# A recurrence kernel: the mixes and the feeds of a tile put together, the projection cut in four

## The chip, the cores and the metric

One core of a Trainium2 chip runs the whole program. The metric is the device time of one execution in microseconds. Before the change it is 2249.52 us, the median of 3 runs (2249.39 to 2250.3).

## The reference

The input is x, 16 sequences of 512 tokens and 256 channels. Two layers run over it, each with a mixer and a feed-forward part behind a residual and a layer norm. Only the third part, the recurrence of layer 1, is touched by the change:

```python
        ms = jnp.mean(jnp.square(tokens), axis=-1, keepdims=True)
        x = tokens * jax.lax.rsqrt(ms + EPS) * norm_w
        x = x.reshape(B, T, H, D)
        a_t = jnp.tanh(a)
        def step(state, x_t):
            state = jnp.tanh(jnp.einsum('bhs,hst->bht', state, a_t) + jnp.einsum('bhd,hds->bhs', x_t, b))
            mixed = jnp.einsum('bhs,hsd->bhd', state, c) + skip[None] * x_t
            return (state, mixed)
        xs = jnp.moveaxis(x, 1, 0)
        _, outs = jax.lax.scan(step, state0, xs)
        return tokens + outs @ w_out.T + b_out
```

There are 16 heads with 16 channels and 64 states each, and 512 steps that must follow each other. The latent attention, the FP4 feed-forward and the channel mix around it are not changed.

## The kernel before, in words

Four stages follow each other: attention, the FP4 feed-forward, the recurrence, the channel mix. Each has its own program for every engine; semaphores are written by hand, and the order of an engine's instructions is the order in which the code emits them. The recurrence runs from about 1530 to 2047 us of the span.

It works on 64 tiles of 128 rows. A tile is 8 time steps (STEPS) of the 16 sequences. The state of all heads fills 4 PSUM banks, split in 2 sides of 2 banks. Step t of a tile goes: `recur` on TensorE multiplies the last state with A for side 0, then for side 1 (L1734, L1737; 8 calls a side, each on a 64x64 tile of the array, each shown as 2 matmul records and 2 weight loads), and ScalarE takes the tanh of each side (L1616) into the state. The next `recur` of a side waits for that tanh. The sums of B times the input were put in the same PSUM banks beforehand.

Around this cycle TensorE has side work for each tile, which sits in slots. A slot has the number at = 2t + q, behind the `recur` of step t and side q; all slots used in the loop are odd, so each stands behind side 1 of a step:

- `mix` (L1786, L1783), 2 calls for the 2 halves c of the channels: state times C for the tile before, on 128x32 tiles of the array. VectorE adds skip times x (outs, L1678).
- `project` (L1765): outs times w_out, 64x64 tiles. VectorE then adds z in two steps (L1692, L1694), takes its statistics (L1696, L1698), GpSimd makes 1/sqrt, and VectorE writes x3 (L1670) at the head of the next tile's work.
- `turn` (L1806): the normalised input of the next tile transposed; VectorE copies it scaled into xT (L1651).
- `inputs`, called the feed here (L1755, L1752): B times xT into the other set of sums for the next tile, on 32x64 tiles of the array, again for 2 halves c.

VectorE's order in a tile is: statistics of a later tile (L1636, L1638), x3, outs twice, xT, the normalisation (L1660), z and its statistics. TensorE's loop body holds 2 tiles. A `Fori` runs it once, then `fill` issues 32 matmuls on a quiet tile (L1774), and a second entry of the same code runs it 30 times more; tiles 0, 63 and 64 stand outside the loop. ScalarE's and VectorE's loops hold 4 tiles. Inside the loop a wait of TensorE counts from a register (`await_count`), outside it from a constant.

The slot table before is one line:

```python
        MIXES, PROJECTS, TURNS, FEEDS = (1, 3), (5, 9), 7, (13, 15)
```

So step 0 has mix 0, step 1 mix 1, step 2 projection 0, step 3 the turn, step 4 projection 1, step 5 nothing, step 6 feed 0, step 7 feed 1.

## Time and profile before

| | |
|---|---|
| median of 3 runs | 2249.52 us |
| the profiled execution, its own time | 2245.83 us |
| its span | 2244.1 us |
| TensorE matmul busy | 2186.6 us, 97% |
| VectorE busy | 1718.1 us, 77% |
| GpSimd busy | 1192.8 us, 53% |
| ScalarE busy | 1060.2 us, 47% |
| granted TensorE clock over the span | 0.993 |
| tanh of the recurrence (L1616) | 1024 instructions, 223 ns each |
| recurrence matmuls on L1734 | 8192 records, 219 ns each |

Busy means the union of an engine's records. On TensorE they overlap heavily: four 64x64 tiles of the array work side by side, a record lasts 219 ns and the next one starts some 14 ns later. So busy time and the duration of a record say little about how long a group of matmuls takes; the distance between starts says it. Times in rows are microseconds from the span's start, and durations of a few hundredths can be read from differences of starts in one view only.

### The profile page before, as it was taken

Reading aid. Unit: us, or ns where it says so; the run is one execution under the profiler, and the core shown is the slowest. Engines: PE = TensorE matmul, PEld = TensorE weight load, DVE = VectorE, ACT = ScalarE, POOL = GpSimd, SP = SyncE. Lnnn points to the kernel's source line nnn. Section 1 sums busy time; section 2 is a strip of 40 time slices with the busy share of each in tenths; the row PEclk is TensorE's granted clock in tenths of the full one; section 3 lists DMA queues with packets and bytes.
Section 4 is the critical chain, followed back from the end, with each engine's and each line's share of the span. In section 5 each row is a group of like instructions: output and inputs, shape, how many; then the busy total and the mean of one; then the engine's idle time right before and its main releaser. Section 6 shows DMA issues by size and latency. Waiting matters only on the chain.

```text
span 2244.1 us, 92167 instructions
## 1 busy us (share of the span) xinstructions
PE 2186.6 (97%) x37362; PEld 1540.2 (69%) x37362; DVE 1718.1 (77%) x4980; ACT 1060.2 (47%) x2707; POOL 1192.8 (53%) x1680
## 2 busy tenths in 40 slices
PE   9999999999999999999999999998999999999997
PEld 5566565656556555556777777777888888887775
DVE  5788888888887777769999999994555555556997
ACT  4655665656666665552222222222444444443444
POOL 4555555655655555536666666674344444442334
PEclk9999999999999999999999999998999999999999
DMA  4111111211121111111210101100011111111232
GB/s 150 58 49 58 67 63 63 67 58 58 67 67 58 68 58 58 50 52 31 68 33 30 33 31 32 42 24 29 28 33 36 34 33 33 37 49 38 87 94 76
DMA packets 101634, 117.83 MB, mean 53 GB/s; under 512 B 10672, under 2 KB 80080, under 8 KB 101456
## 3 DMA queue, kind: packets, MB, share of 16 engines
q1 hardware_dynamic: 101456, 115.44, 15.8%
q8 instruction: 113, 1.85, 0.4%
q14 instruction: 65, 0.53, 0.1%
HBM read 48.29 MB, written 33.55 MB: 36 GB/s over the span
## 4 chain that ended last, share of the span: by engine, by line
PE 92%; DVE 4%; issue 2%; ACT 1%; POOL 0%; DVEq 0%; ACTq 0%; POOLq 0%
PE ps_state L1734 10%; PE ps_down L1373 7%; PE ps_gate L1366 7%; PE ps_up L1366 7%; PE ps_near L812 6%; PE ps_far L592 5%; PE ps_near L584 5%; PE ps_far L584 4%; PE ps_near L592 3%; PE ps_far L627 3%; PE ps_far L611 3%; PE ps_far L604 3%; PE ps_state L1765 3%; PE ps_state L1737 2%; PE ps_r L2152 2%; PE ps_v L2163 2%
## 5 line engine op out<-in xcount | busy, mean ns | idle before, releaser
L1616 ACT ACTIVATE r_state<-ps_state 128x64 f32<-128x64 f32 x1024 | 228.4, 223 | 288.7 <-PE ps_state L1737 283.9
L1734 PE MATMUL ps_state<-r_state,later_pairs_a 64*64 64x32 f32 x8192 | 338.3, 219 | 24.4 <-ACT r_state L1616 11.7
L1734 PEld LDWEIGHTS ps_state<-r_state,later_pairs_a 64*64 64x64 f32 x8192 | 298.2, 135 | 76.1 <-issue 56.3
L1737 PE MATMUL ps_state<-r_state,later_pairs_a 64*64 64x32 f32 x8192 | 334.8, 220 | 1.2 <-issue 1.1
L480 DVE CUSTOM_DVE_ANT_0 ps_near<-ps_near,mask 128x512 f32<-128x512 f32 (+1 forms) x512 | 270.4, 589 | 83.6 <-PE ps_near L584 83.5
L340 POOL TENSOR_SCALAR_AFFINE_SELECT probsT<-probsT 128x512 f32<-128x512 f32 x256 | 160.6, 640 | 266.1 <-ACT probsT L460 168.2
L1737 PEld LDWEIGHTS ps_state<-r_state,later_pairs_a 64*64 64x64 f32 x8192 | 289.7, 135 | 0.4 <-issue 0.4
L480 DVE CUSTOM_DVE_ANT_0 ps_far<-ps_far,mask 128x384 f32<-128x384 f32 (+1 forms) x512 | 198.3, 457 | 33.6 <-PE ps_far L584 32.5
L1256 POOL TENSOR_TENSOR f_fp<-f_rounded,f_scale 128x960 f32<-128x960 f32 (+2 forms) x67 | 117.3, 1751 | 162.7 <-DVE f_rounded L1345 162.7
L1278 ACT ACTIVATE f_silu<-ps_gate 128x704 f32<-128x704 f32 x64 | 48.4, 757 | 285.8 <-PE ps_gate L1366 285.8
L592 PE MATMUL ps_far<-Q,K 32*128 32x256 f32 (+2 forms) x1536 | 181.2, 416 | 1.2 <-ACT probsT L457 0.5
L1373 PE MATMUL ps_down<-kept_w_downT,f_hT 128*128 128x256 f32 x768 | 176.7, 380 | 1.5 <-ACT f_hT L1283 1.5
L460 ACT ACTIVATE probsT<-ps_far 128x512 f32<-128x512 f32 x256 | 132.2, 603 | 90.0 <-PE ps_far L598 90.0
L584 PE MATMUL ps_near<-K,Q 32*128 32x512 f32 (+1 forms) x1024 | 162.7, 518 | 1.7 <-DVE bias_row L498 0.8
L592 PEld LDWEIGHTS ps_far<-Q,K 32*128 32x128 f32 x1536 | 129.6, 184 | 49.6 <-issue 24.7
L1366 PE MATMUL ps_gate<-kept_w_upT,f_xT 128*128 128x352 f32 x512 | 162.1, 460 | 1.4 <-DVE z L487 0.9
L1366 PE MATMUL ps_up<-kept_w_upT,f_xT 128*128 128x352 f32 x512 | 162.1, 460 | 0.0
L1581 POOL TENSOR_TENSOR r_veps<-r_mv,r_eps 128x1 f32<-128x1 f32 x64 | 12.2, 190 | 280.2 <-DVE r_mv L1698 280.2
L1373 PEld LDWEIGHTS ps_down<-kept_w_downT,f_hT 128*128 128x128 f32 x768 | 141.1, 190 | 18.5 <-ACT f_hT L1283 1.9
L812 PE MATMUL ps_near<-probsT,V 128*32 128x512 f32 (+3 forms) x2048 | 151.1, 436 | 0.8 <-ACT probsT L427 0.8
L329 POOL TENSOR_TENSOR k_sin<-K,cos_sin 128x512 f32<-128x512 f32 x64 | 81.1, 1268 | 131.2 <-ACT K L418 131.2
L480 DVE DVE_READ_ACCUMULATOR2_ANT top<- 128x1 f32 x1024 | 142.6, 139 | 0.0
(218 smaller groups left out, 5411.7 us busy)
## 6 DMA issues: line engine op xcount, KB each, us to landing
q_swap<-q_sin SPq DMA_DIRECT2D x128, 128.0 KB, 2.1
k_swap<-k_sin SPq DMA_DIRECT2D x128, 128.0 KB, 2.1
xT<-in_xT_dram SPq DMA_DIRECT2D x16, 512.0 KB, 3.7
xtok<-in_x_dram SPq DMA_DIRECT2D x16, 512.0 KB, 3.8
x_rows<-x SPq DMA_DIRECT2D x16, 512.0 KB, 2.9
f_x<-x_rows SPq DMA_DIRECT2D x64, 128.0 KB, 2.1
x_rows<-f_x SPq DMA_DIRECT2D x64, 128.0 KB, 1.8
r_x<-x_rows SPq DMA_DIRECT2D x64, 128.0 KB, 2.1
```

The costliest lines, as they stand in the source:

```text
L340: return nc.gpsimd.affine_select(block, block, pattern=[[0, GROUP], [1, P]], compare_op=ALU.is_ge, fill=0.0, base=0, channel_multiplier=-1)
L460: nc.scalar.activation(mine[:, t, AT[1]:AT[1] + SEQ], far[t], ACT.Exp).then_inc(exped, 1)
L480: nc.vector.tensor_tensor_reduce(bank[:, at:at + width], bank[:, at:at + width], mask[:, SEQ - width:SEQ], 1.0, -3e38, ALU.add, ALU.max, t ...
L584: out = nc.tensor.matmul(bank[:, at:at + width], Q[rows, g, qi * P:(qi + 1) * P], K[rows, g, 0:width], start=True, stop=True, skip_group_c ...
L592: return nc.tensor.matmul(bank[:, at:at + SEQ - kj * P], K[rows, g, kj * P:(kj + 1) * P], Q[rows, g, kj * P:SEQ], start=(kj != 3), stop=Fa ...
L812: out = nc.tensor.matmul(near[0][LATENT * t:LATENT * (t + 1), kj * P:SEQ], V[:, jp, kj, head_of(gp, t), :], probsT[:, gp % 2, t, AT[kj]:AT ...
L1256: nc.gpsimd.tensor_tensor(blocks(parts(fp4[:, s, :], i, BLOCK)), blocks(parts(rounded[:, s, :], i, BLOCK)), spread(parts(scale[:, s, :], i ...
L1366: out = nc.tensor.matmul(ps[:, half, 0:HALF], xT[:, j % 2, c, :], w_upT[:, c, at + half * HALF:at + (half + 1) * HALF], start=(c == 0), st ...
L1373: out = nc.tensor.matmul(ps_down[:, 0:DIM], hT[:, j % 2, kd, :], w_downT[:, kd, :], start=(kd == 0), stop=(kd == KD - 1))
L1616: nc.scalar.activation(state[:, j % 2, banks, :, t, 0, :], sums[j % 2][:, banks, :, now], ACT.Tanh).then_inc(state_ready[t], 1)
L1734: nc.tensor.matmul(sums[j % 2][half(v), stays, c, now], A[half(v), 3 * q, c, :], last[half(v), stays, c, :], start=False, stop=True, skip_ ...
L1737: out = nc.tensor.matmul(sums[j % 2][half(1 - v), changes, c, now], A[half(v), 3 * q + 1 + was, c, :], last[half(v), changes, c, :], start ...
```

## The change

The two mixes of a tile stand behind each other in slot 1 (step 0). The projection is cut by output columns (n) and by channel half (c) in four pieces of 4 calls with 128 columns, where there were two of 4 calls with 256; the pieces go to slots 3, 7, 9 and 11 (steps 1, 3, 4, 5). The turn goes to slot 5 (step 2), in tile 0 it stays in slot 7. Both feeds stand behind each other in slot 15 (step 7). Steps count from 0 here; step 6 has no side work now. The last tile has its pieces in slots 3, 4, 5 and 6. A piece waits for outs only where n is 0. VectorE's, ScalarE's, GpSimd's and the DMA queues' programs stay as they are. The inner matmuls of the mix stand at L1789 and L1786 in the changed file, the projection at L1768, the turn at L1812.

```diff
--- before.py
+++ after.py
@@ -1756,15 +1756,18 @@
                                              start=(c == 0), stop=False, skip_group_check=True)
             return out
 
-        def project(j, c, states):
-
-            s = (j - 1) % 2
-            await_count(outs_ready, states[c])
+        def project(j, piece, states):
+
+
+            s, n, c = (j - 1) % 2, piece // CC, piece % CC
+            columns = slice(n * P, (n + 1) * P)
+            if n == 0:
+                await_count(outs_ready, states[c])
             for tokens in range(2):
                 for r in range(2):
-                    out = nc.tensor.matmul(room[s][half(tokens), OUT[r], :], outs[half(r), s, c, half(tokens)], w_outT[half(r), c, :],
+                    out = nc.tensor.matmul(room[s][half(tokens), OUT[r], columns], outs[half(r), s, c, half(tokens)], w_outT[half(r), c, columns],
                                            start=(c == 0), stop=(c == CC - 1), skip_group_check=True)
-            if c == CC - 1:
+            if piece == 2 * CC - 1:
                 out.then_inc(out_full, 1)
 
         def fill(j, bank, times, start):
@@ -1786,9 +1789,12 @@
                         nc.tensor.matmul(into, C[:, 3 * (bank // 2), c, :], state[:, s, bank, c, :, 0, :], start=True, stop=True)
             return out
 
-        MIXES, PROJECTS, TURNS, FEEDS = (1, 3), (5, 9), 7, (13, 15)
-
-        LAST_PROJECTS, MIXING = (5, 7), 11
+
+        MIXES, PROJECTS, TURNS, FEEDS = 1, (3, 7, 9, 11), 5, 15
+
+        FIRST_TURNS = 7
+
+        LAST_PROJECTS, MIXING = (3, 4, 5, 6), 11
 
         def first_turn():
 
@@ -1818,32 +1824,29 @@
                     if exists(i, 0):
                         recur(j, t, q, states)
                     at = SIDES * t + q
-                    if at in MIXES and not first:
-                        if at == MIXES[0]:
-                            for side in range(SIDES):
-                                await_count(state_ready[STEPS - 1], states[side])
-                        mix(j, MIXES.index(at)).then_inc(mix_full, 1)
-                    if at == TURNS and exists(i, 1):
+                    if at == MIXES and not first:
+                        for side in range(SIDES):
+                            await_count(state_ready[STEPS - 1], states[side])
+                        for c in range(CC):
+                            mix(j, c).then_inc(mix_full, 1)
+                    if at == (FIRST_TURNS if first else TURNS) and exists(i, 1):
                         await_count(xn_ready, next_tile)
                         await_count(outs_ready, states[1])
                         if first:
                             pe.wait_ge(*fed[1])
                         turn(j)
-                    if at in projects and not first:
-                        project(j, projects.index(at), states)
+                    for piece in range(2 * CC):
+                        if at == projects[piece] and not first:
+                            project(j, piece, states)
                     if at == MIXING and last:
                         pe.wait_ge(z_added, TILES)
                         mixing.to(0)
-                    if at in FEEDS and exists(i, 1):
-                        c = FEEDS.index(at)
-                        if c == 0:
-                            await_count(xT_ready, next_tile)
-                            await_count(z_added, this_tile)
-                            if first:
-                                pe.wait_ge(*fed[1])
-                        out = inputs(j, c)
-                        if c == CC - 1:
-                            out.then_inc(inputs_in, 1)
+                    if at == FEEDS and exists(i, 1):
+                        await_count(xT_ready, next_tile)
+                        await_count(z_added, this_tile)
+                        for c in range(CC):
+                            out = inputs(j, c)
+                        out.then_inc(inputs_in, 1)
 
             for t in range(STEPS):
                 if first and t == LAST_FED:
```

TensorE's rows at the head of the loop, before, from the last matmuls of step 0's `recur` to those of step 1 (L1786 and L1783 are the mix, L1734 and L1737 the recurrence):

```order
L1737 MATMUL ps_state<-r_state,later_pairs_a 64x32 x2
L1786 MATMUL ps_state<-r_state,later_pairs_c 32x128
L1783 MATMUL ps_state<-r_state,later_pairs_c 32x4x16
L1786 MATMUL ps_state<-r_state,later_pairs_c 32x128
L1783 MATMUL ps_state<-r_state,later_pairs_c 32x4x16 x3
L1734 MATMUL ps_state<-r_state,later_pairs_a 64x32 x2
```

The same place in the changed kernel (L1789 and L1786 are now the mix):

```order
L1737 MATMUL ps_state<-r_state,later_pairs_a 64x32 x2
L1789 MATMUL ps_state<-r_state,later_pairs_c 32x128
L1786 MATMUL ps_state<-r_state,later_pairs_c 32x4x16
L1789 MATMUL ps_state<-r_state,later_pairs_c 32x128
L1786 MATMUL ps_state<-r_state,later_pairs_c 32x4x16 x3
L1789 MATMUL ps_state<-r_state,later_pairs_c 32x128
L1786 MATMUL ps_state<-r_state,later_pairs_c 32x4x16
L1789 MATMUL ps_state<-r_state,later_pairs_c 32x128
L1786 MATMUL ps_state<-r_state,later_pairs_c 32x4x16 x3
L1734 MATMUL ps_state<-r_state,later_pairs_a 64x32 x2
```

The second mix moved up past the 16 calls of step 1's `recur` and stands behind the first without a recurrence matmul between.

TensorE's rows around projection 0, before: it stood behind side 1 of step 2 (L1765):

```order
L1734 MATMUL ps_state<-r_state,later_pairs_a 64x32 x2
L1737 MATMUL ps_state<-r_state,later_pairs_a 64x32 x2
L1765 MATMUL ps_state<-later_w_outT,r_outs 64x256 x4
L1734 MATMUL ps_state<-r_state,later_pairs_a 64x32 x2
L1737 MATMUL ps_state<-r_state,later_pairs_a 64x32 x2
```

And in the changed kernel, behind side 1 of step 1:

```order
L1734 MATMUL ps_state<-r_state,later_pairs_a 64x32 x2
L1737 MATMUL ps_state<-r_state,later_pairs_a 64x32 x2
L1768 MATMUL ps_state<-later_w_outT,r_outs 64x128 x4
L1734 MATMUL ps_state<-r_state,later_pairs_a 64x32 x2
L1737 MATMUL ps_state<-r_state,later_pairs_a 64x32 x2
```

A piece has as many calls as a projection had, with half the columns; there are four a tile, so 8 calls more a tile than before.

## Rows read from the trace of the kernel before

**Rows 1.** The page: busy time by engine, and the chain by engine.
```profile
PE 2186.6 (97%) x37362; PEld 1540.2 (69%) x37362; DVE 1718.1 (77%) x4980; ACT 1060.2 (47%) x2707; POOL 1192.8 (53%) x1680
...
PE 92%; DVE 4%; issue 2%; ACT 1%; POOL 0%; DVEq 0%; ACTq 0%; POOLq 0%
```

**Rows 2.** A window of 30 us; busy (records) by engine, PEclk, DMA share, GB/s.
```profile
1571.00:1601.00 30.00, 29.01 (x1371) 25.13 (x1368) 15.14 (x52) 13.39 (x60) 10.04 (x24) 1.00 0.09 27
```

**Rows 3.** ScalarE's timeline: start, length, line, records, idle before; steps 0 to 7, 0.
```profile
1696.23 0.46 ACT L1616 ACTIVATE r_state<-ps_state 128x64 f32<-128x64 f32 x2 [0.93 <-PE ps_state L1737]
1697.15 0.46 ACT L1616 ACTIVATE r_state<-ps_state 128x64 f32<-128x64 f32 x2 [0.46 <-PE ps_state L1737]
1698.11 0.46 ACT L1616 ACTIVATE r_state<-ps_state 128x64 f32<-128x64 f32 x2 [0.50 <-PE ps_state L1737]
1699.01 0.46 ACT L1616 ACTIVATE r_state<-ps_state 128x64 f32<-128x64 f32 x2 [0.44 <-PE ps_state L1737]
1699.87 0.46 ACT L1616 ACTIVATE r_state<-ps_state 128x64 f32<-128x64 f32 x2 [0.40 <-PE ps_state L1737]
1700.77 0.46 ACT L1616 ACTIVATE r_state<-ps_state 128x64 f32<-128x64 f32 x2 [0.44 <-PE ps_state L1737]
1701.63 0.46 ACT L1616 ACTIVATE r_state<-ps_state 128x64 f32<-128x64 f32 x2 [0.40 <-PE ps_state L1737]
1702.69 0.46 ACT L1616 ACTIVATE r_state<-ps_state 128x64 f32<-128x64 f32 x2 [0.61 <-PE ps_state L1737]
1703.79 0.45 ACT L1616 ACTIVATE r_state<-ps_state 128x64 f32<-128x64 f32 x2 [0.64 <-PE ps_state L1737]
```

**Rows 4.** TensorE's timeline around mix 0 (step 0).
```profile
1703.68 0.23 PE L1737 MATMUL ps_state<-r_state,later_pairs_a 64*64 64x32 f32 x2
1703.84 0.30 PE L1786 MATMUL ps_state<-r_state,later_pairs_c 128*32 128x128 f32 x1
...
1703.97 0.27 PE L1786 MATMUL ps_state<-r_state,later_pairs_c 128*32 128x128 f32 x1
...
1704.20 0.25 PE L1734 MATMUL ps_state<-r_state,later_pairs_a 64*64 64x32 f32 x2
```

**Rows 5.** TensorE's timeline around feed 1 (step 7).
```profile
1702.79 0.32 PE L1755 MATMUL ps_state<-r_xT,later_pairs_b 32*64 32x128 f32 x1
...
1702.95 0.27 PE L1755 MATMUL ps_state<-r_xT,later_pairs_b 32*64 32x128 f32 x1
...
1703.20 0.24 PE L1734 MATMUL ps_state<-r_state,later_pairs_a 64*64 64x32 f32 x1
```

**Rows 6.** TensorE's timeline: the turn (step 3), a projection (step 2), recurrence behind each.
```profile
1699.13 0.46 PE L1806 MATMUL ps_state<-kept_ident,r_xn 64*64 64x64 f32 x16
1699.38 0.21 PE L1734 MATMUL ps_state<-r_state,later_pairs_a 64*64 64x32 f32 x1
...
1705.64 0.64 PE L1765 MATMUL ps_state<-later_w_outT,r_outs 64*64 64x256 f32 x8
1706.11 0.20 PE L1734 MATMUL ps_state<-r_state,later_pairs_a 64*64 64x32 f32 x2
```

**Rows 7.** VectorE's timeline: z, x3 and the first outs.
```profile
1700.68 0.41 DVE L1692 TENSOR_TENSOR r_z<-ps_state,r_x_twice 128x256 f32<-128x256 f32 x1
...
1703.31 0.41 DVE L1670 TENSOR_SCALAR r_x<-r_z,r_mv,r_rstd 128x256 f32<-128x256 f32 x1
1704.36 0.35 DVE L1678 SCALAR_TENSOR_TENSOR r_outs<-r_xT,later_recurrence_columns,ps_state 128x128 f32<-128x128 f32 x1 [0.64 <-PE ps_state L1783]
```

**Rows 8.** DMA: PE's code queue q8 in 1541 to 1571; the only one in 1571 to 2013.
```profile
q8 instruction: 6, 0.10, 1.3%
...
q14 instruction: 2, 0.02, 0.0%
```

**Rows 9.** TensorE's timeline: where two stalls of the first pass end.
```profile
1555.32 0.24 PE L1734 MATMUL ps_state<-r_state,later_pairs_a 64*64 64x32 f32 x2 [2.19 <-issue]
...
1565.04 0.19 PE L1737 MATMUL ps_state<-r_state,later_pairs_a 64*64 64x32 f32 x1 [1.06 <-issue]
```

## The prediction

> **What bounds the kernel now.** I read four views in this order. The page: TensorE is busy 97% of the span and 92% of the chain that ended last is PE [rows 1]. That is a busy share of overlapping records, so it does not say whether the recurrence waits for the array or for the loop through ScalarE. The windows: in the recurrence the granted clock is 1.00, its upper level of 2.4 GHz, and 1371 matmul records run in 30 us [rows 2]. The timeline of ScalarE gives the answer. Its tanh pair starts once a step, so the distance of two starts is the length of a step, and what TensorE does between them is known from the slot table. One tile reads 0.92, 0.96, 0.90, 0.86, 0.90, 0.86, 1.06, 1.10 us for steps 0 to 7, 7.56 in all [rows 3]. Step 5 has no side work at all, step 3 has the turn, and both take 0.86. So 0.86 is a floor set by the way PE, ScalarE, PE, and every step above it is set by TensorE's own work: steps 0 and 1 (one mix each), 2 and 4 (one projection each), 6 and 7 (one feed each). Under the floor there is free room on TensorE: the turn occupies it from 1699.13 to 1699.38, 0.25 us, and costs nothing [rows 6].
>
> **The question of the change** is then simple: a piece of side work is free if it fits in a step's room, and costs its full length when the room is already used. Moving work out of a step can win no more than that step's excess over 0.86.
>
> **Projections.** One projection is 8 records of 256 columns, from 1705.64 to the next recurrence matmul at 1706.11: 0.47 us, excess 0.04 (0.90 less 0.86) [rows 3, 6]. A piece has the same 8 records with 128 columns, so about 0.24 us, if it goes by columns as the row's length suggests. That is the turn's size, which is free. Steps 1, 3, 4 and 5 now carry one piece each and step 2 the turn. Bounds for a piece: 0 (the turn) and 0.04 (a whole projection), I take 0. Steps 2 and 4 give back 0.04 each: **-0.08**. The 8 extra calls a tile and their weight loads lie in the same room.
>
> **Mixes.** Before: 0.92 and 0.96. In step 1 the mix goes and a piece comes: 0.96 to 0.86, **-0.10**. Step 0 gets the second mix behind the first. Its price: a mix runs its 128 columns in two passes, first start 1703.84, second pass 1703.97, 0.13 each, so 0.26 for another; with the way out to the next recurrence matmul (1704.20) it is 0.36 [rows 4]. The projection's 0.47 for 256 columns in two passes gives 0.24 for 128. So the bounds are 0.24 and 0.36 and I take 0.26, as the passes are this operation's own: **+0.26**. Nothing hides it: step 0 is already above the floor.
>
> The way from a recurrence matmul into a mix shows 0.16 us between starts (1703.68 to 1703.84) [rows 4]. Merging leaves out one way in and one way out, and the two terms hold this already, because the marginal price has neither in it. What merging wins there is spent again on the floor: the freed step cannot get below 0.86.
>
> **Feeds.** Step 6 falls from 1.06 to the floor: **-0.20**. Step 7 gets the second feed. A feed starts at 1702.79, its second pass at 1702.95, the next recurrence matmul at 1703.20 [rows 5]. Two passes are 0.26 (at 0.13) to 0.32 (at 0.16); outer bounds 0.24 by the projection's columns and 0.41 if merging saved nothing. I take **+0.28**. The two waits ahead of the feeds move to step 7 with them; such a wait at the head of a group is worth 0 to 0.06 (steps 0 and 1 with the same work differ by 0.04), I take **+0.04**.
>
> **Sum of a tile:** -0.08 - 0.10 + 0.26 - 0.20 + 0.28 + 0.04 = **+0.20 us**, so 7.56 becomes 7.76. The cause is plain: before, two rooms swallowed part of a mix and two rooms part of a feed; now one room does in each case, and step 6 stands empty. 60 tiles of the loop run in steady state: 60 x 0.20 = +12.0 us.
>
> **Ends of the loop.** The first two tiles of the loop are held up by code loading: their stalls end at 1555.32 and 1565.04, and by my count of the built program 512 instructions lie between, 9.72 us or 19 ns each [rows 9]; side work is free there. The change adds 8 calls to each of the two tiles in the body, and a call is 2 matmuls and 2 weight loads, so 64 instructions: 1.2 us once, and I put 0.6 us for the last two tiles, whose code is fresh too. Tiles 0 and 64 have no excess that moves. Together **+13.8 us**. The profiled execution took 2245.8 us (span 2244.1); it would become 2259.6. The median of the runs shown lies 3.7 us above it: 2249.5 + 13.8 = **2263.3 us**. A measurement of this kernel can tell about 0.2% (4.5 us) from no change.
>
> **Who waits for whom.** The last piece now ends in step 5, one step later. z starts 0.81 us after the tanh of step 4 (1700.68 against 1699.87), x3 2.63 after z, and x3 runs 0.41 [rows 3, 7]. Moved by a step, x3 ends about 3.7 to 3.85 us after the tanh of step 5; the tanh of the next step 0 comes 0.86 + 0.86 + 1.42 = 3.1 after it, the first outs 0.57 later at 3.7 (1704.36 against 1703.79). So x3 and the first outs, in VectorE's order, just touch. Outs takes 0.35 and is wanted by the first piece 1.2 us after the tanh of step 0: ready at 0.92 to 1.1. Price 0, with little cover; if the cover is gone, the rival below. z itself is ready some 0.3 us before the feeds of step 7 ask for it. The queue behind PE's new wait for outs in step 1 holds the whole recurrence.
>
> **Rivals.**
> 1. **Code of the loop has to be loaded again** (24%). In steady state no packet of PE's code queue is seen, only 2 of 8 KB for others in 442 us, while 6 packets with 0.10 MB, so 16 KB and 256 instructions each, came in the first pass [rows 8]. The stalls mark where blocks begin: the one that ends at 1555.32 stands before instruction 802 of the loop by my count, so blocks begin at 34, 290 and so on to 1570. By that count the old loop and the 32 warming matmuls behind it end within 7 blocks, 5 instructions short of an eighth. The new loop (1561 instructions, it was 1497) still ends 9 short, but the warming block crosses, and the block ahead of it is then fetched too. If that pushes out the loop's first block, the jump back loads again: one block, a stall of 1 to 2.2 us [rows 9], which is 2265; or all of it, (9.72 - 5.6) x 3 = 12 us, which is 2275 (5.6 us is what 512 instructions take in steady state, at 2739 records in 30 us [rows 2]). The Trainium skill, page Runtime: NRT & Kernel Launch, section Instruction fetch mechanics, gives PE 2048 instructions in blocks of 256, and a stall for a taken branch out of them; the trace agrees that a loop of 1497 stays in.
> 2. **The loop itself crosses the edge** (3%). My 9 instructions are wrong and every jump reloads: 30 x 12 us, about 2620.
> 3. **The second group is nearly free** (5%, the faster side). The 0.13 us between the passes of a mix would then be a wait for the array to empty, as the 0.16 us of the way in are, and a second group of the same shape would run inside it: 0.26 less 0.16 is 0.10 for each group, a tile at 0.20 - 0.16 - 0.18 = -0.14, 60 x -0.14 + 1.8 = -6.6, 2242.9. It decides below 0.17 for each group. For it: the ways in and out (0.16 us in, 0.23 from the second pass to the next recurrence matmul) are wider than the 0.13 within. Against it: the projection, which changes no shape, also takes 0.24 for 128 columns in two passes [rows 6]. The Trainium skill, page TensorEngine Tiling (Array Packing), section Key Properties, says that changing the tiling mode drains the engine. By that rule the two merged groups save two drains on the way in and two on the way out, and it speaks for the change; the trace agrees that there is a gap of 0.16 us between 64x64 and 128x32 tiles.
> 4. **VectorE comes late** (8%). The first piece waits for outs, 0.1 to 0.2 us a tile: 2269 to 2275. For it: the touch above. Against: a step with a piece needs TensorE for 0.90 - 0.24 = 0.66 of its 0.86, so step 1 has 0.2 us of room even then.
> 5. **Nearly nothing changes** (5%): groups at 0.20 or less each: +0.06 a tile or less, 2255 or under; nearly all of it within 0.2%. The spacing of starts inside a group, some 10 ns, speaks for it, the passes against it.
>
> **How the numbers follow.** Forecast 55%, 2263.3. With groups at 0.24 a tile costs 0.14 and the time is 2249.5 + 8.4 + 1.8 = 2259.7; the low end goes on into rival 5, as far as groups at 0.20 with +0.06 a tile, 3.6 + 1.8 = 5.4: 2255. The high end takes in rivals 1 and 4 (2275) and groups at 0.36 (+0.38 a tile, 22.8 + 1.8: 2274): 2276. Left out are rivals 2 and 3 and some tails. Faster by over 0.2%: 0.05; within 0.2%: 0.04; slower by over 0.2%: 0.91.
>
> **What would show it.** ScalarE's starts in a new tile: 1.18, then six steps of 0.86, then 1.42, 7.76 in all. Two mixes 0.26 apart and two feeds 0.28 apart. PE's code queue silent again after the warming block. Wrong: step 1 above 0.9 with PE waiting for outs; step 0 at 1.0 (rival 3); 16 KB packets inside the loop (rivals 1, 2); freed steps below 0.8.

## The result, and the profile after

The changed kernel takes 2293.99 us, the median of 4 runs (2291.68 to 2296.67), against 2249.45 us for the kernel before beside it (4 runs, 2247.72 to 2250.3): ratio 1.0204, interval 1.0191 to 1.0218. It is 44.5 us slower. The prediction said slower, but 13.8 us, and its range ended at 2276.

The profiled execution took 2295.57 us (span 2293.8, granted clock 0.984 where it was 0.993). Its page, TensorE's code queue first in the list of queues:

```profile
PE 2223.2 (97%) x38386; PEld 1566.7 (68%) x38386; DVE 1716.6 (75%) x4980; ACT 1064.1 (46%) x2707; POOL 1192.2 (52%) x1680
...
q8 instruction: 122, 2.00, 0.4%
...
PE 92%; DVE 4%; issue 2%; ACT 1%; POOL 0%; DMA 0%; DVEq 0%; ACTq 0%; SPq 0%; POOLq 0%
```

Beside [rows 1] the busy shares and the chain say nothing: PE is 97% and 92% in both. The two things to see are the 1024 matmul records more (8 calls x 2 records x 64 tiles) and 122 packets on q8, TensorE's code queue. The page of before has 113 there:

```profile
q8 instruction: 113, 1.85, 0.4%
```

 Two views find the 44.5 us, one for the loop in steady state and one for its first tiles.

**Steady state.** ScalarE's timeline of a whole pair of tiles (starts of step 7, then 0 to 7, then 0 to 7 of the next tile):

```profile
1684.43 0.46 ACT L1616 ACTIVATE r_state<-ps_state 128x64 f32<-128x64 f32 x2 [0.39 <-PE ps_state L1737]
1686.07 0.43 ACT L1616 ACTIVATE r_state<-ps_state 128x64 f32<-128x64 f32 x2 [1.18 <-PE ps_state L1737]
1687.17 0.46 ACT L1616 ACTIVATE r_state<-ps_state 128x64 f32<-128x64 f32 x2 [0.67 <-PE ps_state L1737]
1688.03 0.46 ACT L1616 ACTIVATE r_state<-ps_state 128x64 f32<-128x64 f32 x2 [0.40 <-PE ps_state L1737]
1688.92 0.46 ACT L1616 ACTIVATE r_state<-ps_state 128x64 f32<-128x64 f32 x2 [0.44 <-PE ps_state L1737]
1689.79 0.46 ACT L1616 ACTIVATE r_state<-ps_state 128x64 f32<-128x64 f32 x2 [0.40 <-PE ps_state L1737]
1690.65 0.46 ACT L1616 ACTIVATE r_state<-ps_state 128x64 f32<-128x64 f32 x2 [0.40 <-PE ps_state L1737]
1691.51 0.46 ACT L1616 ACTIVATE r_state<-ps_state 128x64 f32<-128x64 f32 x2 [0.40 <-PE ps_state L1737]
1692.36 0.46 ACT L1616 ACTIVATE r_state<-ps_state 128x64 f32<-128x64 f32 x2 [0.39 <-PE ps_state L1737]
1694.19 0.23 ACT L1616 ACTIVATE r_state<-ps_state 128x64 f32<-128x64 f32 x1 [1.38 <-PE ps_state L1737]
...
1695.53 0.46 ACT L1616 ACTIVATE r_state<-ps_state 128x64 f32<-128x64 f32 x2 [0.68 <-PE ps_state L1737]
```

The tile from 1686.07 reads 1.10, 0.86, 0.89, 0.87, 0.86, 0.86, 0.85, 1.83 us for steps 0 to 7: 8.12. The next one has 1.34 in step 0 and 1.64 in step 7, 8.16. (The one ends with the loop's jump back in step 7, and part of the jump's cost shows in step 0 of the next.) Over the later tiles of the loop the mean tile is 8.14 us; the same mean before is 7.73, since its tiles are not all as short as the 7.56 of [rows 3]: 0.41 a tile.

**The first tiles.** From the first tanh of a tile to that of the next, tiles 0 to 5 took 11.05, 11.91, 19.50, 7.55, 7.76 and 7.74 us before, 65.5 together; after 11.10, 18.15, 20.28, 17.95, 12.98 and 9.44, 89.9 together. That is 24.4 us more in six tiles, of which 6 x 0.41 = 2.5 belong to the steady price. So about **22 us** are a thing of the loop's start, and about **25 us** (62 x 0.41) the steady price. Of the 22, 16 lie in tiles 3 to 5 (40.4 us where they took 23.1, less 3 x 0.41) and 6 in tiles 1 and 2 (38.4 where they took 31.4, less 2 x 0.41). Windows, after and then before (busy and records by engine; granted clock, DMA share, GB/s):

```profile
1541.00:1571.00 30.00, 22.98 (x785) 20.83 (x768) 8.57 (x29) 8.13 (x34) 6.96 (x18) 0.66 0.10 29
1571.00:1612.00 41.00, 28.66 (x835) 25.28 (x830) 9.12 (x30) 7.56 (x34) 8.53 (x22) 0.71 0.06 17
1612.00:1642.00 30.00, 29.13 (x1360) 25.32 (x1350) 14.37 (x49) 12.88 (x58) 11.18 (x26) 0.94 0.11 34
```

```profile
1541.00:1571.00 30.00, 24.36 (x728) 20.35 (x729) 8.45 (x29) 7.30 (x33) 9.26 (x23) 0.77 0.13 38
1571.00:1612.00 41.00, 39.59 (x1888) 34.35 (x1885) 21.26 (x71) 18.40 (x83) 15.25 (x39) 1.00 0.09 26
```

In the same 41 us from 1571 there are 835 matmul records where there were 1888, and the granted clock is 0.71 instead of 1.00. The DMA queues of after name the reason, in 1541 to 1571, in 1571 to 1612, and all that is left of code loading in 1612 to 2080:

```profile
q8 instruction: 5, 0.08, 1.2%
```

```profile
q8 instruction: 10, 0.16, 1.8%
```

```profile
q14 instruction: 2, 0.02, 0.0%
```

TensorE's code comes in 16 KB blocks on q8. Before, the first pass of the loop brought in the loop's blocks and the one behind them [rows 8], and no packet came after it until the loop's end. Now that block, in which the warming matmuls end, comes at 1571.3, and one more behind it at 1575.2; counted from the one in which the loop begins it is the ninth. Right behind it come eight packets from 1576.7 to 1610.1: the loop's whole code a second time. TensorE's timeline shows the place:

```profile
1571.06 0.61 PE L1777 MATMUL ps_state<-r_quiet 128*128 128x256 bf16 x4
1574.05 4.88 PE L1777 MATMUL ps_state<-r_quiet 128*128 128x256 bf16 x28 [2.39 <-issue]
1580.00 0.25 PE L1734 MATMUL ps_state<-r_state,later_pairs_a 64*64 64x32 f32 x2 [1.06 <-issue]
...
1583.03 0.32 PE L1734 MATMUL ps_state<-r_state,later_pairs_a 64*64 64x32 f32 x2 [2.60 <-issue]
```

The group of warming matmuls (L1777) stops after 4 of its 32 matmuls. By the prediction's count the loop ends 9 instructions short of an edge, and four matmuls with their weight loads are eight. The two rows behind it with a wait for issue are the loop's own head, whose code had been loaded 40 us earlier. So **rival 1 happened**, in its whole form.

### The profile page after: what moved, and what is told of

Same layout as the page of the kernel before. It is cut to its first block, busy times and chain, and to the rows that moved or that the text cites. A ratio compares the mean times of both kernels' runs of the same rounds, so it can differ in the third digit from the quotient of the medians.

```text
span 2293.8 us, 94215 instructions
## 1 busy us (share of the span) xinstructions
PE 2223.2 (97%) x38386; PEld 1566.7 (68%) x38386; DVE 1716.6 (75%) x4980; ACT 1064.1 (46%) x2707; POOL 1192.2 (52%) x1680
## 4 chain that ended last, share of the span: by engine, by line
PE 92%; DVE 4%; issue 2%; ACT 1%; POOL 0%; DMA 0%; DVEq 0%; ACTq 0%; SPq 0%; POOLq 0%
PE ps_state L1734 10%; PE ps_down L1373 7%; PE ps_gate L1366 6%; PE ps_up L1366 6%; PE ps_near L812 6%; PE ps_far L592 5%; PE ps_near L584 5%; PE ps_far L584 4%; PE ps_state L1737 3%; PE ps_state L1768 3%; PE ps_near L592 3%; PE ps_far L627 3%; PE ps_far L611 3%; PE ps_far L604 3%; PE ps_k L2134 2%; PE ps_r L2155 2%
## 5 line engine op out<-in xcount | busy, mean ns | idle before, releaser
L1734 PE MATMUL ps_state<-r_state,later_pairs_a 64*64 64x32 f32 x8192 | 351.3, 221 | 27.4 <-issue 14.2
L1734 PEld LDWEIGHTS ps_state<-r_state,later_pairs_a 64*64 64x64 f32 x8192 | 307.4, 137 | 87.2 <-issue 75.0
L1737 PE MATMUL ps_state<-r_state,later_pairs_a 64*64 64x32 f32 x8192 | 347.4, 222 | 0.0
L1737 PEld LDWEIGHTS ps_state<-r_state,later_pairs_a 64*64 64x64 f32 x8192 | 293.1, 137 | 0.0
L460 ACT ACTIVATE probsT<-ps_far 128x512 f32<-128x512 f32 x256 | 132.5, 605 | 89.9 <-PE ps_far L598 89.9
```

The lines of the kernel that those rows point to most:

```text
L460: nc.scalar.activation(mine[:, t, AT[1]:AT[1] + SEQ], far[t], ACT.Exp).then_inc(exped, 1)
L1734: nc.tensor.matmul(sums[j % 2][half(v), stays, c, now], A[half(v), 3 * q, c, :], last[half(v), stays, c, :], start=False, stop=True, skip_ ...
L1737: out = nc.tensor.matmul(sums[j % 2][half(1 - v), changes, c, now], A[half(v), 3 * q + 1 + was, c, :], last[half(v), changes, c, :], start ...
```

## The experiments

A step's length below is the distance of ScalarE's starts in steady state, a pair's length the distance from the first row of a group of side work to the next recurrence row on TensorE. "Ahead of the loop" always means this edit, which moves all code behind it by n/2 instructions (two waits become one):

```diff
+        for _ in range(n):
+            pe.wait_ge(set_up, 1)
         with pe.Fori(0, 2) as again:
```

| kernel | median us (runs) | ratio to before, interval |
|---|---|---|
| the change | 2293.99 (4) | 1.0204, 1.0191 to 1.0218 |
| a_pad40 | 2301.95 (4) | 1.0294, 1.0214 to 1.0374 |
| a_pad100 | 2276.86 (4) | 1.0132, 1.0117 to 1.0147 |
| a_fill0 | 2266.16 (4) | 1.0079, 1.0064 to 1.0095 |
| a_feed8 | 2249.84 (8) | 1.0010, 1.0000 to 1.0020 |
| a_feed16 | 2275.59 (2) | 1.0123, 1.0105 to 1.0142 |
| a_feed10 | 2272.64 (1) | |
| a_feed12c | 2273.65 (1) | |
| b_feeds | 2262.96 (4) | 1.0070, 1.0050 to 1.0089 |
| b_mixes | 2253.93 (7) | 1.0036, 1.0023 to 1.0050 |
| b_pad12 | 2250.54 (10) | 1.0021, 1.0011 to 1.0031 |
| b_pad60 | 2255.53 (12) | 1.0046, 1.0026 to 1.0067 |
| b_pad100 | 2249.72 (11) | 1.0010, 1.0002 to 1.0019 |
| b_spread | 2253.32 (11) | 1.0023, 1.0014 to 1.0032 |
| b_spread_fill0 | 2247.60 (11) | 1.0006, 0.9995 to 1.0017 |
| b_fill0 | 2243.04 (12) | 0.9981, 0.9971 to 0.9991 |

### Where the blocks of code lie

**a_pad40**: the change with n = 40 ahead of the loop.

> The changed kernel with 40 waits that are long satisfied ahead of TensorE's loop, so that by the count of instructions the loop and the warming matmuls behind it end within seven blocks of 256 (the loop begins at place 6 of a block, ends at 1567, the warming block at 1633 of 1792). Theory A (the jump back out of the warming block found the loop's first blocks thrown out, and all of it was loaded again): the code packets of TensorE in 1541 to 1620 fall from 17 to about 8, tiles 3 and 4 run at 8.1 to 8.2 us, and the time falls by 18 to 25 us, to 2269 to 2276. Rival B (the slow first tiles come from the change's own order in code that is fresh): the packets and the time stay within 4 us of 2294.

The edit is 20 instructions and not 40 as the expectation counts (94235 in the trace, 94215 in the change). So it is not the test that was meant: the crossing isn't taken away, the loop itself now ends 11 behind the edge. Measured: 2301.95 us (one of four runs at 2335.39, hence the wide interval), 8 us more than the change, and 122 packets on q8 as in the change: the reload is there, with eight packets from 1578.3 to 1613.5 behind a ninth block at 1575.3. The first six tiles take 99.7 us together, 9.8 more than in the change. Its queue list for 1625 to 2080, where the loop runs in steady state, has no q8 at all:

```profile
q1 hardware_dynamic: 16896, 15.47, 10.8%
q14 instruction: 1, 0.01, 0.0%
```

So a loop that runs over the edge into an eighth block (14 instructions, six whole blocks, 11 instructions) does not load again at every jump; its mean tile is 8.13 us, as in the change. Rival 2 of the prediction would have been false even where its premise holds. A loop over nine blocks wasn't run.

**b_pad12**: the kernel before with n = 12 ahead of the loop.

> The kernel before with 12 satisfied waits ahead of the loop: the warming block now crosses into an eighth block by 7 instructions, the loop itself does not. Theory A: 16 KB packets go on after the warming block, tiles 3 to 5 are slow, and the time rises by 15 to 25 us to 2265 to 2275. Rival B: twelve waits cost under 1 us, 2249 to 2251.

Six instructions, so the warming matmuls with the jump behind them cross the edge by one. 2250.54 us and 113 packets on q8: nothing loaded again. Its mean tile is 7.80 us instead of 7.73, which makes the 4 us; the difference lies in the steps with the jump back.

**a_pad100**: the change with n = 100, by which the loop starts on place 16 and nothing crosses.

> The changed kernel with 50 instructions of satisfied waits ahead of TensorE's loop (two waits made one instruction, so the earlier run with 40 waits moved the blocks by 20 only and pushed the loop itself over an edge). Now the loop begins at place 16 of a block and the warming matmuls end at 1643 of 1792. Theory A (whole reload once, after the warming block has crossed into an eighth block and a ninth was fetched): 17 code packets in 1541 to 1620 fall to 8, tiles 3 to 5 run at 8.0 to 8.2 us from the start, 19 to 25 us less than the changed kernel, 2269 to 2275. Rival B (the slow tiles 3 to 5 belong to the change's order): within 4 us of 2294.

2276.86 us, 17.1 less than the change, though 50 instructions were added; 113 packets on q8. Tiles 3 to 5 take 24.1 us together, 16 less than in the change, and the mean tile is 8.02 us where it was 8.14, which is 7 us more; tile 0 gives back 6, as it takes 16.9 us behind the added instructions. In the window in which the change had 835 matmul records and a clock of 0.71:

```profile
1571.00:1612.00 41.00, 38.20 (x1568) 32.46 (x1568) 16.69 (x56) 14.60 (x66) 13.40 (x32) 0.89 0.09 27
```

This shows that the reload hangs on where the code lies, not on the order of the work.

**b_pad60**: the kernel before with n = 60; the warming matmuls with their jump cross by 25.

> The kernel before with 30 instructions of satisfied waits ahead of the loop: the loop ends inside the seventh block, the warming block crosses by 25 instructions (with 6 instructions, by one, nothing was loaded again). Theory A: eight more 16 KB packets behind the warming block, tiles 3 to 5 slow, 15 to 25 us more, 2262 to 2272. Rival B: 2247 to 2252.

2255.53 us, with a mean tile of 7.82 us, and the profiled execution has 113 packets and no reload, against the expectation. One of the 12 runs took 2282.66 us, 27 above the median; it wasn't profiled, so whether it was a reload stays open. In the change they cross by 59 (5 short before, and 64 instructions more). In the traces the reload goes with a ninth block, counted from the one in which the loop begins, fetched before the loop is entered again (both executions with 122 packets), and crossing by few instructions fetches no ninth block. Where the border between 25 and 59 lies wasn't tried.

**b_pad100**: the kernel before with n = 100.

> The kernel before with 50 instructions of satisfied waits: loop at place 16, warming block ends at 1579 of 1792, nothing crosses. Theory A: no packet after the warming block, and the first pass as before. The edges of the blocks move within the loop, and the time of the jump back (0.42 us a pair of tiles before, 0.33 to 0.56 in the runs so far) may move by 0.15 either way: 2242 to 2254.

2249.72 us: nothing gained and nothing lost within the bound. Its steady tile is 7.67 us instead of 7.73, as a stall of 0.256 us at the head of every fourth tile is gone, but its first tile takes 16.7 us instead of 11.05. Between a_pad100 and b_pad100, both without crossing and with the loop at the same place, the steady difference is 8.02 - 7.67 = **0.35 us a tile**, and the whole difference 27.1 us: 20 in the 56 tiles behind the first six, 5 in the first six, the rest at the ends. That is the price of the change itself, clear of where its code lies.

**a_fill0**: the change without the 32 warming matmuls. The line stands in the outer loop, so it takes out two groups, the one between the two entries and a second one behind the loop.

```diff
-            fill(0, TURN[0], 32, False)
```

> The changed kernel without the 32 warming matmuls behind each pass of the outer loop. The loop then ends 7 instructions short of the edge and nothing enters the eighth block. Theory A: no whole reload, 17 us less as in a_pad100, and the two groups of warming matmuls, 5 and 4 us, fall away too: 2268 to 2275, if the clock recovers by itself within a few tiles. Rival B (reload has nothing to do with the warming block): 2285 to 2290.

2266.16 us, 27.8 below the change, 113 packets on q8. Tiles 0 to 3 take 11.1, 17.87, 12.02 and 8.26 us, and the tile behind the loop 8.00 where it took 11.44: the second group alone is 3.4 us. Nothing crosses now, so nothing loads again, and the clock in the second window is at its upper level without the warming matmuls:

```profile
1571.00:1612.00 41.00, 38.77 (x1868) 33.31 (x1868) 20.41 (x69) 17.89 (x80) 16.57 (x40) 1.00 0.10 33
```

The whole differences, 17.1 and 27.8 us, hold other things beside the reload. Tiles 3 to 5 price it alone: 40.4 us in the change, 24.1 in a_pad100, 24.5 in a_fill0, so **16 us** from either side. The other 6 of the loop's 22 lie ahead of it, and tile 1 makes them: it takes 18.15 us in the change and 17.87 in a_fill0, where before it took 11.91, so the first pass is slow with the reload and without. The granted clock was lower there than before (0.66 against 0.77 in 1541 to 1571), and a_pad100 has 14.8 with the same calls; why wasn't tried. Tile 2, which holds the stalls of 2.39 and 1.06 us shown above, is only 0.8 longer than before.

### What each part of the change costs

**b_mixes**: the kernel before with both mixes in slot 1. (Of the diffs here and below only the main lines are shown.)

```diff
-        MIXES, PROJECTS, TURNS, FEEDS = (1, 3), (5, 9), 7, (13, 15)
+        MIXES, PROJECTS, TURNS, FEEDS = 1, (5, 9), 7, (13, 15)
```

> The kernel before with the mixes alone put together in slot 1. Forecast by the columns' passes: step 0 +0.26, step 1 from 0.96 to 0.86, +0.16 a tile, +10 us, 2259. By what the changed kernel shows (step 0 +0.19, and +0.1 more where the loop jumps back): +0.1 to 0.15 a tile, +6 to 9 us, 2255 to 2259.

2253.93 us, +0.10 us a tile. Step 1 is 0.86, step 0 is 1.13 in the tile that begins without the jump. The pair of mixes in the change, to be read against [rows 4]:

```profile
1686.08 0.30 PE L1789 MATMUL ps_state<-r_state,later_pairs_c 128*32 128x128 f32 x1
...
1686.33 0.27 PE L1789 MATMUL ps_state<-r_state,later_pairs_c 128*32 128x128 f32 x1
...
1686.67 0.25 PE L1734 MATMUL ps_state<-r_state,later_pairs_a 64*64 64x32 f32 x2
```

From 1686.08 to 1686.67 are 0.59 us, where one mix took 0.36: the second costs 0.23. The second mix starts 0.25 behind the first. The predicted 0.26 stands almost as put.

**b_feeds**: the kernel before with both feeds in slot 15.

```diff
-        MIXES, PROJECTS, TURNS, FEEDS = (1, 3), (5, 9), 7, (13, 15)
+        MIXES, PROJECTS, TURNS, FEEDS = (1, 3), (5, 9), 7, 15
```

> The kernel before with the feeds alone put together in slot 15 (loop length 1497, no crossing). If the second feed costs what the changed kernel shows, step 6 falls by 0.16 to 0.21 and step 7 rises by 0.45 to 0.54, +0.3 us a tile, 60 tiles: +18 us, 2267 to 2268. If merged feeds cost only their columns (my forecast, +0.12 a tile): +7 us, 2257.

2262.96 us, +0.22 us a tile: by far the dearer part. Step 6 falls to 0.85, but step 7 takes 1.60 in one tile and 1.84 in the other. TensorE's timeline of the change around the pair, to be read against [rows 5]:

```profile
1684.39 0.21 PE L1737 MATMUL ps_state<-r_state,later_pairs_a 64*64 64x16 f32 x2
1684.64 0.29 PE L1755 MATMUL ps_state<-r_xT,later_pairs_b 32*64 32x128 f32 x1
...
1685.27 0.28 PE L1752 MATMUL ps_state<-r_xT,later_pairs_b 32*64 32x64 f32 x5
1685.48 0.25 PE L1734 MATMUL ps_state<-r_state,later_pairs_a 64*64 64x32 f32 x2
```

From 1684.64 to 1685.48 are 0.84 us; one feed took 0.41 [rows 5]. The second feed costs 0.43 us, as much as the first one with its way out, though it has no way out of its own. The way in, 0.25 us here, holds the two waits.

The two parts alone come to 0.32 us a tile, the whole change to 0.41, or to 0.35 with the blocks aligned alike. So the projection in four pieces and the moved turn, which were to give back 0.08, give back nothing that this sum shows. It can't show 0.04, though: where the code lies alone moves the mean tile by up to 0.15 (7.67 to 7.82 with n = 0 to 100).

### Why the second feed costs 0.43

A feed has 12 calls: banks 0 and 2 take one call of 128 columns for each v (2 each), banks 1 and 3 two calls of 64 strided columns, by parity (4 each). Four kernels change only that.

**a_feed8**: all four banks in whole calls; the exchange by parity of banks 1 and 3 is left out.

```diff
-                        if bank % 2:
-                            out = nc.tensor.matmul(steps_of(sums[s][half(v ^ parity), bank, c, :], parity), B[rows, 2 * c + v, :], steps_of(xT_now, parity),
-                                                   start=(c == 0 and parity == 0), stop=False, skip_group_check=True)
-                        elif parity == 0:
-                            nc.tensor.matmul(sums[s][half(v), bank, c, :], B[rows, 2 * c + v, :], xT_now,
-                                             start=(c == 0), stop=False, skip_group_check=True)
+                        if parity == 0:
+                            out = nc.tensor.matmul(sums[s][half(v), bank, c, :], B[rows, 2 * c + v, :], xT_now,
+                                                   start=(c == 0), stop=False, skip_group_check=True)
```

> The changed kernel with 8 calls of 128 columns in each feed in place of 12 (4 of 128, 8 of 64): the parity exchange of every second bank is left out, so these banks get their inputs in the wrong order; the columns that stream through each tile of the array are the same, 128 a feed. Theory C (the second feed is bound by how fast instructions come, 9 ns each): it costs 32 x 9 = 0.29 us in place of 0.43, and step 7 falls by 0.14 to 0.25 as the first feed shrinks too. Rival D (bound by columns or by draining): step 7 unchanged within 0.04. The loop is 64 instructions shorter and crosses nothing, so tiles 3 to 5 are not slow.

```profile
1697.23 0.70 PE L1752 MATMUL ps_state<-r_xT,later_pairs_b 32*64 32x128 f32 x32
1697.97 0.25 PE L1734 MATMUL ps_state<-r_state,later_pairs_a 64*64 64x32 f32 x2
```

These rows are of a tile with the jump back: 0.74 us from the first row of the pair to the recurrence, where the change takes 1.16; in the tile without it it is 0.63, where the change takes 0.84. The last start is 0.43 behind the first. Step 7 is 1.40 and 1.43, and the kernel takes 2249.84 us, 27 less than a_pad100, as much as the kernel before. 17 of the 27 are the steady tiles (7.72 us against 8.02); the rest lie in the loop's first tiles and at its end (this kernel has fewer instructions and no added waits). The tile with the jump wins most: 1.84 to 1.43. So split calls are a good part of what makes the merged feeds dear. What a second feed of whole calls costs behind a first is not measured, as no kernel here has one such feed alone.

**a_feed16**: all four banks in split calls (n = 40 ahead of the loop; with the calls added ahead of it the loop begins on place 50, so nothing crosses).

```diff
-                        if bank % 2:
-                            out = nc.tensor.matmul(steps_of(sums[s][half(v ^ parity), bank, c, :], parity), B[rows, 2 * c + v, :], steps_of(xT_now, parity),
-                                                   start=(c == 0 and parity == 0), stop=False, skip_group_check=True)
-                        elif parity == 0:
-                            nc.tensor.matmul(sums[s][half(v), bank, c, :], B[rows, 2 * c + v, :], xT_now,
-                                             start=(c == 0), stop=False, skip_group_check=True)
+                        to = v ^ parity if bank % 2 else v
+                        out = nc.tensor.matmul(steps_of(sums[s][half(to), bank, c, :], parity), B[rows, 2 * c + v, :], steps_of(xT_now, parity),
+                                               start=(c == 0 and parity == 0), stop=False, skip_group_check=True)
```

> The changed kernel with 16 calls of 64 columns in each feed in place of 12 calls, the same columns and the same result, and 20 instructions of waits ahead of the loop so that nothing crosses (17 code packets fall to 9). Against a_pad100 (step 7 of an odd tile 1.60 us): Theory C (the supply of instructions, 9 ns each): 2 x 16 instructions more, step 7 at 1.85 to 1.90, 15 to 20 us more than a_pad100, 2292 to 2297. Rival D (columns or draining): step 7 at 1.60 to 1.64, 2277 to 2280.

```profile
1701.10 0.92 PE L1752 MATMUL ps_state<-r_xT,later_pairs_b 32*64 32x64 f32 x64
1701.95 0.25 PE L1734 MATMUL ps_state<-r_state,later_pairs_a 64*64 64x32 f32 x2
```

0.85 us for 16 calls a feed where 12 took 0.84. A third more instructions cost nothing in this tile, so the supply of instructions is not the limit there. In the tile with the jump back the pair takes 1.21 us for 1.16, and the mean tile is 8.07 for 8.02.

**a_feed12c**: 12 calls, but banks 1 and 3 are split in the first and the second 64 columns instead of by parity, so they get other inputs (n = 100).

```diff
+                        part = half(parity)
...
-                            out = nc.tensor.matmul(steps_of(sums[s][half(v ^ parity), bank, c, :], parity), B[rows, 2 * c + v, :], steps_of(xT_now, parity),
+                            out = nc.tensor.matmul(sums[s][half(v ^ parity), bank, c, part], B[rows, 2 * c + v, :], xT_now[:, part],
```

> The changed kernel with the same 12 calls of a feed, but the split calls take 64 columns that lie side by side instead of every second group of 16 (the banks with an exchange get wrong inputs), and 50 instructions of waits so that nothing crosses. Theory E: the pair still spans 0.66 to 0.70. Theory F (the strided reading or writing of the split calls is what costs): 0.43 to 0.50, and the time falls by 10 us or more against a_pad100's 2276.9.

2273.65 us (a single run), and the pair's last start lies 0.70 us behind its first, exactly as in the change. The stride is not the reason.

**a_feed10**: bank 3 whole, bank 1 split: 10 calls a feed.

```diff
-                        if bank % 2:
+                        if bank == 1:
```

> The changed kernel with 10 calls in a feed: bank 1 keeps its two calls of 64 columns a half, bank 3 gets one call of 128 (its parity exchange is left out, so its inputs are in the wrong order). The pair of feeds spans 0.697 us from first to last start with 12 and with 16 calls and 0.43 with 8. Theory E (the strip of 32 rows with most weight loads sets it: 8 a feed in a strip with split calls, 4 in one without): 0.66 to 0.70, as one strip still has 8. Theory G (the number of calls above 8): 0.56 to 0.60.

The last start is 0.59 to 0.62 us behind the first, the kernel takes 2272.64 us (a single run). With 0, 1, 2 and 4 banks split the same distance is 0.43, 0.59, 0.70 and 0.70 us. The theory of the busiest strip (0.66 to 0.70) falls by this, and that of the number of calls (0.56 to 0.60) fits here but not at 16 calls. So the split lengthens the pair, and how it does so stays open.

### Spreading instead of merging

If merging costs, cutting the feed finer could win. **b_spread** puts the 24 feed calls of a tile in three groups of 8, in slots 11, 13 and 15 of the kernel before (steps 5, 6, 7).

```diff
-        MIXES, PROJECTS, TURNS, FEEDS = (1, 3), (5, 9), 7, (13, 15)
+        MIXES, PROJECTS, TURNS, FEEDS = (1, 3), (5, 9), 7, (11, 13, 15)
...
+        PARTS = ([p for p in EVERY if p[2] % 2 and p[0] == 0],
+                 [p for p in EVERY if not p[2] % 2 and p[0] == 0] + [p for p in EVERY if p[2] % 2 and p[0] == 1 and p[1] == 0],
+                 [p for p in EVERY if not p[2] % 2 and p[0] == 1] + [p for p in EVERY if p[2] % 2 and p[0] == 1 and p[1] == 1])
```

> The kernel before with the same 24 feed calls of a tile in three groups of 8, in slots 11, 13 and 15 (slot 11 takes banks 1 and 3, whose readers are done; z is waited for at slot 13), the opposite of putting them together. Theory (each step has free room, and a group pays only what goes over it): step 5 rises from 0.86 to 0.88 to 0.95, steps 6 and 7 fall by 0.09 to 0.14 each, -0.1 to -0.2 us a tile, 6 to 12 us less than before, 2237 to 2243. Rival (each group of another array shape pays its way in and out, 0.16 us and more, so a third group costs what it saves): within 4 us of before.

2253.32 us, 0.2% slower, against the expectation and as its rival had it. ScalarE's starts of steps 5, 6, 7 and the next 0:

```profile
1692.23 0.46 ACT L1616 ACTIVATE r_state<-ps_state 128x64 f32<-128x64 f32 x2 [0.44 <-PE ps_state L1737]
1693.23 0.46 ACT L1616 ACTIVATE r_state<-ps_state 128x64 f32<-128x64 f32 x2 [0.54 <-PE ps_state L1737]
1694.19 0.46 ACT L1616 ACTIVATE r_state<-ps_state 128x64 f32<-128x64 f32 x2 [0.51 <-PE ps_state L1737]
1695.25 0.42 ACT L1616 ACTIVATE r_state<-ps_state 128x64 f32<-128x64 f32 x2 [0.60 <-PE ps_state L1737]
```

They are 1.00, 0.96 and 1.06, together 3.02, where before they are 0.86, 1.06 and 1.10 [rows 3], also 3.02. A group of 8 calls starts 0.15 us behind the recurrence, runs 0.18 between its first and last start and needs 0.20 to the next recurrence row: 0.53, where 12 calls need 0.56. Two thirds of a small group are its ways in and out, so a third of the work less saves nearly nothing. (The group in slot 11, all of split calls, runs 0.24 and needs 0.15 behind it: 0.54.) Spreading ends where the ways outweigh the work. The mean tile is 7.79 us against 7.73, and the longest step is step 0 behind the jump (1.16 for 1.04), where the placing of the code acts too.

**b_spread_fill0**, the same without the warming matmuls:

> The feeds in three groups and no warming matmuls. If the clock recovers by itself: 5 to 8 us under b_spread. If the recurrence stays at the lower clock without them: steps of 1.28 us as in the slow tiles, far above 2300.

2247.60 us, 5.7 less than b_spread, at the same mean tile (7.79). The gain is that of the warming matmuls alone, which the last kernel takes up.

### A version that beats both

**b_fill0**: the kernel before without the line `fill(0, TURN[0], 32, False)`.

> The kernel before without the 32 warming matmuls behind each of the two passes of the outer loop; nothing else. With the feeds in three groups their removal gave 5.7 us (2253.3 to 2247.6), and steps came down from 1.28 to 0.86 within two tiles by themselves. The same here: 5 to 7 us less than before, about 2241.

2243.04 us, ratio 0.9981 (0.9971 to 0.9991), 5 us less than the kernel before beside it. Tiles 0 to 4 take 11.05, 13.33, 15.60, 10.79 and 7.81 us, and in steady state all is as before (7.73). The first six tiles come to 66.3 us where they were 65.5, and the tile behind the loop takes 7.62 where it took 11.10. The clock lies a little lower at first than in the kernel before (0.94 against 1.00) and is at 1.00 from 1612 on:

```profile
1571.00:1612.00 41.00, 39.49 (x1821) 34.11 (x1813) 21.01 (x70) 18.01 (x80) 15.82 (x39) 0.94 0.08 26
```

So in the two profiled executions the first group, 5.3 us long, about pays for itself. What is saved is the second group behind the loop, 3.5 us, which stands there since the line is in the outer loop, and which the clock did not need: it is at 1.00 before it and behind it, with the group and without. The profiled executions differ by 2.9 us and the medians by 5.0; what the first group is worth by itself wasn't run.

## Why the prediction was right and wrong

The direction held, and so did its reason, that a room of its own swallows part of each mix and each feed. The size failed in two places, a rival that was put at 24% and left out of the forecast, and one term of the sum. Without the reload the change takes 2276.86 us (a_pad100), which is still above the forecast's 2263.3 and just above its range. The means of both tiles of the pair, in us, from ScalarE's starts; the last column is b_pad100 to a_pad100, with the code at the same place:

| step | predicted | measured (before to after) | code placed alike |
|---|---|---|---|
| 0, second mix | +0.26 | +0.24 (0.98 to 1.22) | +0.21 |
| 1 | -0.10 | -0.10 (0.96 to 0.86) | -0.10 |
| 2, the turn instead of a projection | -0.04 | 0 (0.90 to 0.89) | 0 |
| 3 and 5, a piece each | 0 | 0 (0.86) | 0 |
| 4 | -0.04 | -0.04 (0.90 to 0.86) | -0.04 |
| 6 | -0.20 | -0.19 (1.04 to 0.85) | -0.19 |
| 7, second feed and the waits | +0.32 | +0.50 (1.24 to 1.74) | +0.48 |
| a tile | +0.20 | +0.41 | +0.35 |

- **The floor and the freed steps** were right: four steps with a piece or with nothing stand at 0.85 to 0.87, none below. A piece of 128 columns is free, as taken.
- **The turn** was taken to be free in step 2 as it is in step 3 [rows 6]. It isn't quite: 0.89. It reads 0.86 in step 3 before, where the step ahead of it was itself held up by a projection; that this hid a part of the turn is the likeliest reading, and it wasn't tried by itself. It is 0.04 us a tile.
- **"I take +0.28"** for the second feed is the term that failed. It measured 0.43. The outer bound of 0.41, "if merging saved nothing", was written down and passed over in favour of two passes of 0.13. With 0.43 in the sum the tile comes to +0.35; the turn adds 0.04 and the mix takes off 0.03, which makes 0.36 for the 0.35 with the code placed alike. The error of method: the price was built from parts of a row group instead of taken from the group as a whole. In the mix, which has whole and split calls in the same proportion (2 and 4, where a feed has 4 and 8), the same method gave 0.26 for 0.23. Why it holds there and not for the feed, whose own starts span 0.27 us when it stands alone and add 0.43 behind another, stays open.
- **Where the code lies** had no term in the steady price, and it is the other 0.06. With 50 instructions ahead of the loop the mean tile falls by 0.06 in the kernel before (7.73 to 7.67) and by 0.12 in the change (8.14 to 8.02). The jump back itself costs about the same in both. TensorE's rows at it, before and then after:

```profile
1648.63 0.28 PE L1752 MATMUL ps_state<-r_xT,later_pairs_b 32*64 32x64 f32 x5
1649.13 0.25 PE L1734 MATMUL ps_state<-r_state,later_pairs_a 64*64 64x32 f32 x2 [0.23 <-issue]
```

```profile
1693.11 0.28 PE L1752 MATMUL ps_state<-r_xT,later_pairs_b 32*64 32x64 f32 x5
1693.62 0.25 PE L1734 MATMUL ps_state<-r_state,later_pairs_a 64*64 64x32 f32 x2 [0.23 <-issue]
```

  That is 0.50 and 0.51 us, where the same rows of the tile without the jump lie 0.21 apart (1685.27 to 1685.48, above). In a_feed8 the jump costs 0.12; why wasn't tried.
- **Rival 1** (24%) came true, and the reload makes 16 us of the miss. Its count of instructions was right: the stall stands behind the fourth warming matmul, and the reload went through eight blocks. Its price for a whole reload, (9.72 - 5.6) x 3 = 12, was near: the second pass took 30.9 us (tiles 3 and 4) where three times 9.72 gives 29.2, at a granted clock of 0.68 where the stretch of 9.72 had 0.65, and the next tile took 1.3 us more than a steady one. What it lacked lies ahead of the reload: tiles 1 and 2 took 7.0 us more, where the forecast put 1.2 for fresh code. The Trainium skill, page Runtime: NRT & Kernel Launch, section Instruction fetch mechanics, has PE hold 2048 instructions in blocks of 256; the trace agrees with eight resident blocks (113 packets against 122, nine more with the ninth block), and so does a_pad40, whose loop lies in eight. The same section says that a taken branch out of the current window of two pages stalls; a_pad40 jumps back over seven blocks with no q8 packet in 455 us and the change's own mean tile, so that doesn't hold here, and the measurement decides.
- **Rival 2** (3%) is false by a_pad40. **Rival 3** (second group nearly free, 0.10) is false: 0.23 and 0.43. The ways in and out of a group are there in every kernel (0.15 and 0.15 to 0.20 us), and merging leaves one of each out, but the second group's own calls run 0.23 and 0.43 all the same. The Trainium skill, page TensorEngine Tiling (Array Packing), section Key Properties, has the engine drain at a change of tiling mode; the trace agrees as far as those ways go, and it does not make the merged pair cheap. **Rival 4** (VectorE late) is false. In VectorE's timeline of the change x3 begins as soon as GpSimd's value is there, and both outs run in one piece:

```profile
1685.74 0.41 DVE L1670 TENSOR_SCALAR r_x<-r_z,r_mv,r_rstd 128x256 f32<-128x256 f32 x1 [0.23 <-POOL r_rstd L1583]
1686.61 0.61 DVE L1678 SCALAR_TENSOR_TENSOR r_outs<-r_xT,later_recurrence_columns,ps_state 128x128 f32<-128x128 f32 x2 [0.45 <-PE ps_state L1786]
```

  The outs wait for the mix and not for x3, and step 1, in which the first piece asks for them, stays at 0.86. **Rival 5** (nothing changes) is false.
- **The median against the profile**: the steady 25 us and the 22 us of the start make 47; the two profiled executions differ by 49.7 and the medians by 44.5, as the profiled execution of before lay 3.7 below its median.

## What to carry to other kernels

Where steps stand on a latency floor, spread the side work until each piece fits its room and no further: a second group behind the first pays its own calls in full (0.23 and 0.43 us here), and a split one pays its ways in and out. Price such a group by the whole stretch from its first row to the next recurrence row (0.36 and 0.41 here) until a run shows less. And count the code: a loop can fit in the blocks that the engine keeps while 28 matmuls behind it, entered once, make it load whole again; a page's packet count on the code queue (113 against 122) shows it at a glance. Compare two orders of a loop with the code at the same place: the placing alone was worth up to 0.15 us a tile.

## What the hardware showed unexpectedly

- A loop of 1561 instructions that lies over eight blocks loads nothing in steady state (a_pad40), while fetching a ninth block between two entries of the loop brought all eight again, at 16 us. Crossing by 1 or 25 instructions did not do so in the profiled executions; one unprofiled run at 2282.66 us leaves that open.
- Code blocks arrive every 4 to 6.5 us in the first pass of the loop, which runs at about half pace (tiles of 11 to 20 us); the granted clock is low beside it (0.66 and 0.71 in the windows above), and once the matmuls were dense it came back to 1.00 with the warming matmuls and without them.
- Two calls of 64 columns in place of one of 128 lengthen a pair of feeds from 0.43 to 0.70 us between first and last start, whether half or all of the banks are split and whether the halves are strided or not. With one bank in four split it is 0.59 to 0.62. No theory tried here gives all four numbers.
